# Window attention after a state-space block: score products over the columns and rows that hold data, values loaded ahead of scores, scores moved by halves

## The reference

```python
xn = batchnorm(x)                                   # over batch, y, x
q, k, v = split(conv1x1(xn, qkv_w, qkv_b))          # each 4 x 6 heads x 16 x 32 x 32
qk = concat([q * 16 ** -0.5, k], axis=channels)     # 24 images (batch x head), 32 channels
attn = conv2d(qk, dm_w, pad=3) + dm_b               # 7 x 7 window, 49 outputs per pixel
attn = softmax(attn + rel_bias, axis=the 49 outputs)
out = sum over k of patches7x7(v)[k] * attn[k]      # the 49 shifted values, weighted
x1 = x + conv1x1(out, proj_w, proj_b)
return x1 + conv1x1(gelu(conv1x1(x1, c1_w, c1_b)), c2_w, c2_b)
```

## Time and profile before

| | |
|---|---|
| median of the three runs | 1193.46 us (1192.46 to 1195.16) |
| the profiled execution, its own time | 1198.2 us |
| its span, first to last instruction | 1196.4 us |
| mean granted TensorE clock | 0.944 |
| TensorE busy | 1073.9 us, 90% |
| VectorE busy | 920.1 us, 77% |
| GpSimd busy | 919.3 us, 77% |
| ScalarE busy | 572.2 us, 48% |
| attention stage | from about 758 us to the end |

### The profile page before, as it was taken

How to read it: one execution, slowest core, us unless ns; L and a number is a source line. 1 busy time by engine, 2 the same in 40 slices (tenths; PEclk the granted TensorE clock), 3 DMA queues, 4 the chain that set the end, 5 groups by cost and what they waited for, 6 DMA issues and landing times. The chain is left out here.

```text
span 1196.4 us, 9538 instructions
## 1 busy us (share of the span) xinstructions
PE 1073.9 (90%) x3268; PEld 376.1 (31%) x3268; DVE 920.1 (77%) x598; ACT 572.2 (48%) x601; POOL 919.3 (77%) x371
## 2 busy tenths in 40 slices
PE   7889999799998999998987979699999999997675
PEld 2223333233333333333332323233333333332221
DVE  1299998779998899998989899400587796969871
ACT  5766858697777654867675644211121121011311
POOL 0089999979998979998999998100298877989880
PEclk8879999899999999999998999699999999998787
DMA  3234566544475545664546474343938476473402
GB/s 84 93 127 157 178 179 158 186 134 157 163 191 146 176 145 147 173 199 154 169 169 176 129 224 157 83 104 73 201 74 184 89 171 116 116 132 58 91 0 75
DMA packets 111042, 165.65 MB, mean 138 GB/s; under 512 B 63411, under 2 KB 76441, under 8 KB 110993
## 3 DMA queue, kind: packets, MB, share of 16 engines
q1 hardware_dynamic: 108880, 157.81, 48.9%
q10 hardware_dynamic: 2112, 7.23, 2.1%
HBM read 137.43 MB, written 11.23 MB: 124 GB/s over the span
## 5 line engine op out<-in xcount | busy, mean ns | idle before, releaser
L749 POOL TENSOR_TENSOR hc<-h,c_rep 128x1024 f32<-128x1024 f32 x191 | 447.5, 2359 | 103.4 <-DVE h L802 91.3
L802 DVE TENSOR_TENSOR_SCAN h<-a,bu 128x1024 f32<-128x1024 f32 x192 | 436.9, 2284 | 32.9 <-ACT bu L630 10.0
L451 PE MATMUL y_ps<-hc,ident 128*128 128x512 f32 x768 | 378.4, 617 | 0.8 <-DVE hc L850 0.3
L620 ACT ACTIVATE a<-dt,a_neg 128x1024 f32<-128x1024 f32 x192 | 216.5, 1143 | 132.1 <-DVE h L802 126.9
L1231 POOL TENSOR_TENSOR prod_p<-vw,at 128x3584 f32<-128x3584 f32 x18 | 130.4, 7242 | 122.8 <-DMA vw<-v_d 116.9
L789 DVE TENSOR_TENSOR bu<-bu,u 128x1024 f32<-128x1024 f32 x165 | 199.7, 1210 | 21.9 <-PE bu L421 21.7
L451 PEld LDWEIGHTS y_ps<-hc,ident 128*128 128x128 f32 x768 | 144.5, 195 | 202.9 <-issue 182.1
L1112 PE MATMUL sc_ps<-x,w_up 128*64 128x512 f32 x672 | 177.9, 604 | 1.2 <-DMA x<-qk 1.2
L1112 PE MATMUL sc_ps<-x,w_low 96*64 96x512 f32 x672 | 177.5, 603 | 0.0
L1182 ACT ACTIVATE sc<-sc_ps,rel 128x512 f32<-128x512 f32 x24 | 16.5, 688 | 257.4 <-PE sc_ps L1112 257.4
L421 PE MATMUL bu<-st,pick 96*128 96x512 bf16 (+1 forms) x438 | 101.7, 390 | 37.8 <-DVE h L802 36.3
(11 more groups left out here) (130 smaller groups left out, 992.6 us busy)
## 6 DMA issues: line engine op xcount, KB each, us to landing
c_rep<-bc_d SPq DMA_DIRECT2D x128, 512.0 KB, 4.0
c_rep<-bc_d SPq DMA_DIRECT2D x128, 256.0 KB, 4.1
vw<-v_d SPq DMA_DIRECT2D x24, 532.0 KB, 9.1
x<-qk SPq DMA_DIRECT2D x66, 171.0 KB, 5.3
b_rep<-bc_d SPq DMA_DIRECT2D x17, 512.0 KB, 5.0
b_rep<-bc_d SPq DMA_DIRECT2D x20, 256.0 KB, 5.2
scores_d<-sc ACTq DMA_DIRECT2D x24, 196.0 KB
at<-scores_d SPq DMA_DIRECT2D x24, 196.0 KB, 3.4
```

The source lines that it names most:

```text
L451: mm = pe.matmul(y_ps[:, cols(th)], ident[:, :], hc[:, k % HC_RING, cols(th)], start=(n == 0 and d == 0), stop=(n == N_ST - 1))
L620: nc.scalar.activation(a[:, k % A_RING, :], dt[:, tile % 2, :], ACT.Exp, scale=a_neg[:, kind_of(tile), n:n + 1]).then_inc(exp_done, 1)
L749: nc.gpsimd.tensor_tensor(hc[:, k % HC_RING, :], h[:, k % H_RING, :], c_rep[:, k % C_RING, :], ALU.mult).then_inc(hc_done, 1)
L802: nc.vector.tensor_tensor_scan(scan_order(h[:, k % H_RING, :], d), scan_order(a[:, k % A_RING, :], d), scan_order(bu[:, k % 2, :], d), 0.0 ...
```

## The change

Five things change together.

1. `qk` and `x4` have no side columns: rows of 32. Each product takes only the output columns whose input column lies in the image (`lo:hi`), so 29 to 32 of 32, and the lower product of the second half only 15 rows (`height`); `x4` holds 35 rows instead of 36. The products of a half go over all `dx` with `w_up`, `dx = 3` first, and then over all with `w_low`, in reverse.
2. Scores are stored and loaded by halves, each with its own semaphore. ScalarE issues the two stores of a half right behind its drain.
3. The values of tile `j` are loaded by `load_values(j)`, issued with pair `2j - 1`, behind its scores and copies; those of tile 0 before any scores.
4. GpSimd waits for `normed` before it first writes `acc_p` in a tile, and not before its first product.
5. The drain of (1, 0) moves in tile 5 from before row 1 to before row 0.

```diff
-X4_ROWS = H + 4
+X4_ROWS = H + 3
+DX_ORDER = (R, 0, 1, 2, 4, 5, 6)
-DVE_MLP = {(4, WIN): ((0, 0),), (4, WIN + 1): ((0, 8),), (5, 1): ((1, 0),), (5, 2): ((1, 8),), (5, 3): ((2, 0),),
+DVE_MLP = {(4, WIN): ((0, 0),), (4, WIN + 1): ((0, 8),), (5, 0): ((1, 0),), (5, 2): ((1, 8),), (5, 3): ((2, 0),),
            (5, WIN): ((2, 8),)}
...
-        qk = sb("qk", [128, 2, 2, HP, HP])
+        qk = sb("qk", [128, 2, 2, HP, W])
-        x4 = sb("x4", [128, X4_RING, X4_ROWS, HP])
+        x4 = sb("x4", [128, X4_RING, X4_ROWS, W])
...
-            def load_tile(j):
-
+            def load_scores(p, th):
+
+                j, rows = p // 2, slice(HALF * th, HALF * th + HALF)
+                if j >= 2 and p % 2 == 0 and th == 0:
+                    sp.wait_ge(pv, pv_before(j - 1))
+                    sp.wait_ge(pp, pp_before(j - 1))
+                sp.wait_ge(sc_stored[p % 2][th], 32 * (p // 2 + 1))
                 for i in range(2):
-                    sp.wait_ge(sc_stored[i], 32 * (j + 1))
+                    y = 64 * (p % 2) + 32 * i + 16 * th
+                    sp.dma_start(at[y:y + 16, j % 2, :, :],
+                                 scores_d[2 * p + i, :, rows].rearrange("k (y x) -> y k x", x=W))\
+                        .then_inc(at_in[j % 2], 16)
+
+            def load_values(j):
+
                 if j >= 2:
                     sp.wait_ge(pv, pv_before(j - 1))
                     sp.wait_ge(pp, pp_before(j - 1))
-                for i in range(4):
-                    sp.dma_start(at[32 * i:32 * i + 32, j % 2, :, :],
-                                 scores_d[4 * j + i].rearrange("k (y x) -> y k x", x=W)).then_inc(at_in[j % 2], 16)
...
             store_v(0)
+            load_values(0)
             for p in range(PAIRS):
-                if p % 2:
-                    load_tile(p // 2)
+                for th in range(2):
+                    load_scores(p, th)
                 if p + 3 < PAIRS:
                     put_x4(p + 3)
                 if p % 3 == 0 and p // 3 + 1 < B:
                     store_v(p // 3 + 1)
-                if p % 2 == 0 and p >= 4:
-                    store_o(p // 2 - 2)
-                    if p // 2 - 2 == LAST_TILE[0]:
-                        load_o(0)
+                j = (p + 1) // 2
+                if p % 2 and j < TILES:
+                    load_values(j)
+                    if j >= 2:
+                        store_o(j - 2)
+                        if j - 2 == LAST_TILE[0]:
+                            load_o(0)
...
-                    for dx in range(WIN):
-                        for w, rows, y0 in ((w_up, 128, 0), (w_low, 96, 4)):
-                            for i in range(2):
-                                y = 16 * th + y0
-                                mm = pe.matmul(sc_ps[64 * i:64 * i + 64, th, :], w[:, dx, :],
-                                               x4[0:rows, (2 * p + i) % X4_RING, y:y + 16, dx:dx + W],
-                                               start=(dx == 0 and y0 == 0), stop=(dx == WIN - 1 and y0 == 4))
+                    taps = [(w_up, 128, 0, dx) for dx in DX_ORDER] + [(w_low, 96, 4, dx) for dx in reversed(DX_ORDER)]
+                    for n, (w, rows, y0, dx) in enumerate(taps):
+                        lo, hi = max(R - dx, 0), min(W + R - dx, W)
+                        height = 15 if th == 1 and y0 == 4 else 16
+                        y = 16 * th + y0
+                        for i in range(2):
+                            out = sc_ps[64 * i:64 * i + 64, th, :].rearrange("p (y x) -> p y x", x=W)
+                            mm = pe.matmul(out[:, 0:height, lo:hi], w[:, dx, :],
+                                           x4[0:rows, (2 * p + i) % X4_RING, y:y + height, dx + lo - R:dx + hi - R],
+                                           start=(n == 0), stop=(n == len(taps) - 1))
...
-                    if p >= 2 and th == 0:
-                        act.wait_ge(sc_stored[p % 2], 32 * (p // 2))
+                    if p >= 2:
+                        act.wait_ge(sc_stored[p % 2][th], 32 * (p // 2))
                     nc.scalar.activation(sc[:, p % 2, cols(th)], sc_ps[:, th, :], ACT.Identity,
                                          bias=rel[:, p % 3:p % 3 + 1]).then_inc(sc_out, 1)
+                    act.wait_ge(sc_out, 2 * p + th + 1)
+                    for i in range(2):
+                        act.dma_start(scores_d[2 * p + i, :, cols(th)], sc[64 * i:64 * i + K2, p % 2, cols(th)])\
+                            .then_inc(sc_stored[p % 2][th], 16)
                     if p % 2 == 0 and p and th == 0:
                         exps(p // 2 - 1)
-                act.wait_ge(sc_out, 2 * p + 2)
-                for i in range(2):
-                    act.dma_start(scores_d[2 * p + i], sc[64 * i:64 * i + K2, p % 2, :]).then_inc(sc_stored[p % 2], 16)
...
             if first:
+                if j:
+                    pool.wait_ge(normed, j)
                 nc.gpsimd.tensor_tensor(acc_p[:, :, :], prod_p[:, 0], prod_p[:, 1], ALU.add).then_inc(pp, 1)
...
-            for lo in (0, R + W):
-                nc.gpsimd.memset(rows[:, :, R:R + H, lo:lo + R], 0.0)
...
-                    if n == 0 and j:
-                        pool.wait_ge(normed, j)
...
-                dve.wait_ge(at_in[j % 2], 64 * (j // 2 + 1))
+                dve.wait_ge(at_in[j % 2], 128 * (j // 2 + 1))
```

More of the change, by code:

```diff
@@ L930, in attention @@
         sc_out = sem("sc_out")
-        sc_stored = [sem(f"sc_stored{i}") for i in range(2)]
+        sc_stored = [[sem(f"sc_stored{i}_{th}") for th in range(2)] for i in range(2)]
         v_stored = [sem(f"v_stored{b}") for b in range(B)]
@@ L1166, in qkv @@
                             act.wait_ge(s, 16 * 8 * (b - 1))
-                    dst = qk[0:rows, m, b % 2, R + y0:R + y0 + 16, R:R + W]
+                    dst = qk[0:rows, m, b % 2, R + y0:R + y0 + 16, :]
                 else:
@@ L1232, in product, with fold_p @@
                                         ALU.mult)
-        def fold_p(pool, base, first):
+        def fold_p(pool, j, base, first):
             for n, (lo, hi) in enumerate((((0, 3), (4, 7)), ((0, 2), (2, 4)))):
@@ L1266, in _ @@
                             prod_p[:, :, :, :]).then_inc(pp, 1)
-                    fold_p(pool, base + 1, n == 0)
+                    fold_p(pool, j, base + 1, n == 0)
         @block.vector
```

## The result

The changed kernel takes 1157.43 us (median of four runs, 1155.66 to 1160.85) against 1194.31 us before: a ratio of 0.969, 95% interval 0.966 to 0.972. The forecast was 1167, range 1161 to 1180: the sign and the kind of gain were right, and some 8 to 10 us of it were missing.

A forecast was written before the change was run, and what follows sets the result against it. TensorE's score products were taken to set the pace up to tile 4, then a fixed tail. T7 14.0 us earlier, with the shorter ways after it, put the join 27.0 earlier: 1193.5 - 27.0 = 1166.5, say 1167, range 1161 to 1180.

The forecast's parts named there:

- What bounds the kernel: Attention stage: TensorE's score products set the pace up to tile 4, then a tail of VectorE, ScalarE and GpSimd.
- The score products: TensorE: fewer columns save 1.7 us a pair, bounds 0.86 to 1.82, with odd starts still costing 0.04 us a group.
- T7: Time when ScalarE has drained pair 7's second half; forecast to fall by 14.0 us, to 981.2.
- The start: Before the first score product: smaller first copy to `x4` saves 0.4 us, bounds 0 to 0.7; removed side memsets save 0.
- Halves and values: From T7 to GpSimd's tile 3: scores by halves and values loaded ahead save 8.0 us, values about 5.7 a tile.
- way of 15.2 us from drain to exponential: Last half's drain to the end of its tile's exponential: 15.2 us instead of 17.5, bounds 12.4 to 17.5.
- The MLP at row 0: VectorE in tile 5: no wait for (1, 8), `den` to join 45.2 us instead of 50.1, bounds 0 and -4.9.
- The normed wait: GpSimd multiplies before VectorE has joined the tile before; worth 0 in the tail, where the exponential is last.
- PSUM gaps: Rival: gapped output costs TensorE 0.04 to 0.08 us a group, a pair saves 0.9 to 0; 1173 to 1181, chance 0.21.
- a slower TensorE: Rival: gapped groups cost over 0.12 us each, making TensorE slower than before; over 1192 us, chance 0.06.
- halves that don't shorten the way: Rival: drain to exponential stays 17.5 us, all 2.3 later, 1169; chance 0.12 shared with MLP or values falling short.
- hidden values: Rival: loading `vw` was hidden anyway, tile 3's 5.7 us not gained, 1173; chance 0.12 shared with halves or MLP.

The follow-up runs named there:

- e5: Changed kernel with one column fewer in the products of `dx` 4 and `dx` 6 (scores lack a part); three pairs took 67.03 us.
- e11: Changed kernel with output, input or both in jumps in upper products of `dx` 1, 5, 2 (scores partly wrong); these groups took 0.43, 0.89, 1.66 us.
- e4: Changed kernel with `x4` and `qk` in rows of 38 with side columns again, products still trimmed; three pairs took 69.05 us.
- e12: Changed kernel with untrimmed 512-column products in the old order and `qk`, `x4` in rows of 40; three pairs took 73.91 us.
- e13: Changed kernel with `qk` and `x4` in rows of 34, data in columns 0 to 31, products trimmed; three pairs took 68.33 us.
- e8: Changed kernel with the two removed side memsets back on GpSimd, into their own tile; first score product at 17.75 us instead of 16.84.
- e0: The changed kernel run again without any edit; 1159.13 us, ratio 0.971 against the kernel before.
- e7: Changed kernel with scores stored by whole images and loaded by tiles, as before the change, values still ahead; 1163.57 us.
- e6: Changed kernel with the values of a tile loaded right behind its own scores, as before the change; 1162.16 us.
- e2: Changed kernel with the first part undone (rows of 38, side columns, untrimmed products in the old order); 1182.07 us, ratio 0.990 against the kernel before.
- e14: Changed kernel with the drain of (1, 0) back before row 1 of tile 5; attention stage ended at 406.3 us, 3.0 later than e0.
- e9: Changed kernel with GpSimd's wait for `normed` back ahead of its first product; attention stage ended at 404.4 us, 1.1 later than e0.

## Why the prediction was off

- **What bounds the kernel**: right. TensorE set the pace up to tile 3, and the tail went as drawn: tile 4 behind tile 3, tile 5 behind ScalarE's Gelus (3.2 us of idle, forecast 3.6), join by VectorE with GpSimd just before it.
- **The score products**: the step that failed. The mechanism, fewer columns, was right; the term "I take 1.7" (bounds 0.86 to 1.82) measured 2.13 a pair, which over eight pairs to T7 is 3.4 us. The forecast carried the 0.04 us of an odd start over to the new rows, and made room for a price of gaps in PSUM. Neither is there: in the changed kernel `dx` 4, from column 1 and with gaps, takes the time of its columns; e5 adds an even length from an odd start, e11 a fully scattered output. Without these two (0.12, and 0.04 for 8 groups = 0.32) the forecast's own sum gives 2.14. The 0.04 belongs to the reading of rows at a pitch of 38 (e4; 0.025 at 40 in e12, up to 0.02 at 34 in e13), and the change of pitch, which I priced only as shorter copies, removed it. Trimming alone at a pitch of 38 leaves 23.02 us a pair, 1.6 less than before, within the forecast's bounds; the pitch gives the other 0.53.
- **The start**: 2.2 us and not 0.4; memsets 0.9 (e8), the rest the shorter copies and the way to the first product. The forecast's 0 for the removed side memsets, "under other work", was wrong.
- **The first pair** runs in part at the lower clock. After start and pace, 0.3 us remain at T7 in the changed kernel and 1.6 in e0; there the pair took 23.28 us for 24.62, which is 1.3 of them.
- **Halves and values**: 8.8 against 8.0 together. The split was off: each undone alone, halves cost 3.4 to 4.0 for 2.3 (e7), values 3.1 for 5.7 (e6), so that the sum came close with one term too low and the other too high. The way of 15.2 us from drain to exponential was added up from store, load, maximum and subtraction; it measured 14.3, and ScalarE's order, not this sum, ended it. That e2 measured just 15.2 is luck: the order set it there too, at the old pace.
- **The MLP at row 0**: -5.4 to -5.9 for -4.9 in the sum; undone by itself it costs 3.0 (e14). The forecast took only the wait for (1, 8) away, 4.7 us; the rest is mostly the shorter wait for (2, 8), 1.62 in the changed kernel and 2.15 in e0 for 2.72.
- **The normed wait**: 1.1 to 2.0 for 0 (e9).
- **The rivals**: PSUM gaps, a slower TensorE, halves that don't shorten the way and hidden values are all refuted. The range ended at 1161 because the forecast case was bounded by 1.82 a pair, below the 2.13 that came, and little was left for the start.

These pieces make 35 us; 1.8 more between the two profiles lie ahead of the stage and are scatter.

## What to carry to other kernels

A bound taken from a row holds only for the layout of that row. Where an edit changes the pitch of the rows that TensorE reads, price it again: compare neighbouring offsets in the old trace, ask what a pitch of 128 bytes would do, the one at which 29 to 32 columns were free here (160 bytes, in e12, were not), and let the gain reach to all columns at full pace. Ask also what stands ahead of a piece of work in its engine's own stream: once the data come early, that order is what is left to wait for. And count from the stage's own first instruction when the stage ahead scatters by more than the effect that you look for.

## What the runs showed of the hardware

- A group of two float32 products of 29 to 32 columns by 16 rows takes the time of its columns when the rows lie at a pitch of 32 words: 0.78, 0.80, 0.83 and 0.86 us. 28 columns from column 3 took 0.77, 0.02 more than theirs (e5). At 34, 38 and 40 words some runs take 0.01 to 0.04 us more.
- Reading one word out of each 128-byte row doubles a product (0.89 us for 0.43); writing PSUM in the same jumps costs nothing (0.43).
- While a GpSimd memset of 2.5 us ran, a VectorE scaling did not end: it ended 0.16 us after the memset in three kernels, having taken 0.57, 1.41 and 1.50 us.
- The attention stage, behind a stage that is the same in all kernels, began anywhere from 751.4 to 758.0 us in the profiles read.
